# Graph attention on Trainium2: the softmax weights also in a PSUM bank of their own

## What is computed

```python
h = jnp.einsum('nf,fhd->nhd', x, W)            # 8 heads of 32
a_src = jnp.sum(h * att_src, axis=-1)
a_dst = jnp.sum(h * att_dst, axis=-1)
e = jax.nn.leaky_relu(a_src[src] + a_dst[dst], 0.2)
e_max = jax.ops.segment_max(e, dst, num_segments=N)
e_exp = jnp.exp(e - e_max[dst])
denom = jax.ops.segment_sum(e_exp, dst, num_segments=N)
msg = h[src] * (e_exp / (denom[dst] + 1e-16))[:, :, None]
out = jax.ops.segment_sum(msg, dst, num_segments=N)
```

## Time and profile before

| what | us |
|---|---|
| median of 3 runs | 3578.84 |
| the profiled execution's own time | 3577.81 |
| its span, first to last instruction | 3576.0 |
| PE busy (70%) | 2496.1 |
| POOL busy (56%) | 1996.6 |
| DVE busy (44%) | 1589.6 |
| ACT busy (37%) | 1310.4 |
| attention: first gather starts | 116.2 |
| attention: last gather starts | 1197.0 |

### The profile page before, as it was taken

The page is one execution under the profiler, slowest core; times in us unless marked ns, Lnnn a source line. Parts: engine busy times, 40 slices in busy tenths (PEclk is TensorE's granted clock), DMA queues, the critical chain, the costliest instruction groups (busy, mean ns, idle before and its releaser), DMA issues. The chain is left out here.

```text
span 3576.0 us, 51073 instructions
## 1 busy us (share of the span) xinstructions
PE 2496.1 (70%) x12468; PEld 1994.8 (56%) x12469; DVE 1589.6 (44%) x3485; ACT 1310.4 (37%) x2826; POOL 1996.6 (56%) x2005
## 2 busy tenths in 40 slices
PE   5466556666665552999924888878888878639993
PEld 4244444444444351888824676767777754427772
DVE  5455555555555582111156444444444454621114
ACT  5443333333333231544443333333222324624441
POOL 0577777777777356222204777777777730463331
PEclk9687888888887755999967999999999989769996
DMA  5444444444444235222255555555555520242226
GB/s 158 124 132 129 129 129 129 129 129 129 127 128 128 67 107 211 75 83 83 78 188 158 158 157 157 157 158 158 156 155 155 156 57 2 95 163 84 87 89 245
DMA packets 319924, 459.47 MB, mean 128 GB/s; under 512 B 56729, under 2 KB 213962, under 8 KB 319498
## 3 DMA queue, kind: packets, MB, share of 16 engines
q0 software_dynamic: 94560, 261.75, 24.6%
q1 hardware_dynamic: 212888, 180.18, 16.9%
q10 hardware_dynamic: 12276, 15.62, 1.3%
HBM read 376.96 MB, written 80.39 MB: 128 GB/s over the span
## 5 line engine op out<-in xcount | busy, mean ns | idle before, releaser
L604 POOL DMA_INDIRECT room<-h_table,src_idx x784 | 843.2, 1075 | 351.5 <-issue 238.2
L2170 POOL DMA_INDIRECT em_msg<-xn_table,src_idx x784 | 746.7, 952 | 337.2 <-issue 238.5
L1100 PE MATMUL at_ps<-room,at_member 128*128 128x264 f32 x1584 | 497.1, 468 | 74.1 <-DVE room L958 65.3
L2246 PE MATMUL em_pse<-em_We,em_attr_t 128*128 128x256 f32 x1552 | 398.4, 415 | 157.5 <-DVE em_msg L2194 157.5
L2194 DVE TENSOR_TENSOR em_msg<-em_pse,em_msg 128x1024 f32<-128x1024 f32 x196 | 230.9, 1220 | 548.1 <-DMA em_msg<-xn_table,src_idx 548.1
L2299 ACT ACTIVATE em_msg<-em_msg 128x1024 f32<-128x1024 f32 x196 | 207.2, 1057 | 681.5 <-DVE em_msg L2194 674.3
L2246 PEld LDWEIGHTS em_pse<-em_We,em_attr_t 128*128 128x128 f32 x1552 | 313.8, 207 | 226.3 <-DVE em_msg L2194 168.3
L1100 PEld LDWEIGHTS at_ps<-room,at_member 128*128 128x128 f32 x1584 | 342.9, 228 | 156.1 <-DVE room L958 82.4
L2253 PE MATMUL em_psa<-em_msg,em_member 128*128 128x256 f32 x1584 | 359.8, 381 | 3.2 <-DVE acc L2204 3.2
L2253 PEld LDWEIGHTS em_psa<-em_msg,em_member 128*128 128x128 f32 x1584 | 302.6, 191 | 44.4 <-DVE acc L2204 3.6
L1070 PE MATMUL at_pst<-ident,at_score 128*128 128x128 f32 x49 | 23.1, 472 | 349.3 <-DVE at_score L888 349.3
(11 more groups left out here) (397 smaller groups left out, 4048.1 us busy)
## 6 DMA issues: line engine op xcount, KB each, us to landing
em_attr<-in_edge_attr_dram SPq DMA_DIRECT2D x97, 512.0 KB, 4.2
room<-x_sorted SPq DMA_DIRECT2D x105, 258.0 KB, 2.7
at_dst_row<-dst_flat SPq DMA_DIRECT2D x98, 256.0 KB, 3.7
room<-h_table,src_idx POOLq DMA_INDIRECT x784
at_resets<-reset_flat SPq DMA_DIRECT2D x784, 8.0 KB
em_msg<-xn_table,src_idx POOLq DMA_INDIRECT x784, 2.8
room<-in_x_dram SPq DMA_DIRECT2D x12, 896.0 KB, 10.2
cn_rows<-y_table SPq DMA_DIRECT2D x5, 1792.0 KB, 10.2
```

What stands on the lines that cost most here:

```text
L604: pool.indirect_dma_start(msg[:, s, j, :], None, mem.h_table[:, :], bass.IndirectOffsetOnAxis(ap=mem.src_idx[:, c:c + 1].bitcast(u32), axi ...
L1100: ins = nc.tensor.matmul(ps_a[:, which, 0:MSG], member[which][:, j, :], msg[:, s, c, :], start=(j == 0), stop=(j == CB - 1))
L2170: pool.indirect_dma_start(msg[:, s, j, :], None, mem.xn_table[:, :], bass.IndirectOffsetOnAxis(ap=mem.src_idx[:, c:c + 1].bitcast(u32), ax ...
L2246: ins = nc.tensor.matmul(ps_e[h][:, j, :], attr_t[:, s % 2, c * P:(c + 1) * P], We[:, :], start=True, stop=True)
```

## The change

`ps_a` gives up its third bank, and `ps_w` takes it. ACT writes the weights twice: first into `ps_w` (its first 128 columns, chunk by chunk with the heads inside, semaphore `weight_out`), then into `msg` as before. `weigh` waits for the first copy, and takes its second operand from `ps_w` instead of from `msg`. The further windows' sums go to columns 8 to 271 of `ps_r`. New waits keep the order: `shift_scores` waits for the last weights in `msg`, PE's first product of a step does so too, and in the last step `spread_scale` waits for the first `weigh`.

```diff
-        ps_a = ctx.enter_context(nc.psum_tensor("at_ps", [P, 3, 512], fp32))
+        ps_a = ctx.enter_context(nc.psum_tensor("at_ps", [P, 2, 512], fp32))
+        ps_w = ctx.enter_context(nc.psum_tensor("at_psw", [P, 512], fp32))
...
+        sums = [ps_a[:, 0, 0:MSG], ps_a[:, 1, 0:MSG], ps_r[:, HEADS:HEADS + MSG]]
+        weight_row = ps_w[:, 0:P]
...
             def shift_scores(k, s, i):
                 dve.wait_ge(turned_back, k + 1)
+                if not isinstance(k, int) or k > 0:
+                    dve.wait_ge(weighted, k)
...
             def weigh(k, s, quarter):
-                dve.wait_ge(weighted, k + 1)
+                dve.wait_ge(weight_out, k + 1)
                 part = msg[:, s, quarter * HC:(quarter + 1) * HC, :].rearrange("p c (h w) -> p (c h) w", w=HW)
+                of_part = weight_row[:, quarter * HC * HEADS:(quarter + 1) * HC * HEADS]
                 nc.vector.tensor_tensor(part[:, :, 0:HD], part[:, :, 0:HD],
-                                        part[:, :, HD:HW].to_broadcast([P, HC * HEADS, HD]), ALU.mult).then_inc(msg_done, 1)
+                                        of_part.unsqueeze(2).to_broadcast([P, HC * HEADS, HD]), ALU.mult).then_inc(msg_done, 1)
...
             def spread_scale(k):
                 pe.wait_ge(scale_ready, k + 1)
                 pe.wait_ge(first_ready, 2 * k + 1)
+                if not has(1, k):
+                    pe.wait_ge(msg_done, 4 * k + 1)
...
             def first_half(k, s, p, half):
                 if half == 0:
                     pe.wait_ge(first_ready, 2 * k + p + 1)
                     pe.wait_ge(first_out, 2 * k + p + 1)
+                    if p == 0:
+                        pe.wait_ge(weighted, k + 1)
...
             def weights(k, s):
                 act.wait_ge(shifted, 2 * k + 2)
+                nc.scalar.activation(weight_row.rearrange("p (c h) -> p h c", h=HEADS), shift[:, :, :], ACT.Exp).then_inc(weight_out, 1)
                 nc.scalar.activation(weight_col(s), shift[:, :, :], ACT.Exp).then_inc(weighted, 1)
```

## The result

The changed kernel takes 3488.52 us (median of 4 runs, 3486.38 to 3492.24) against 3580.1 us for the kernel before (with one run more than above: 4 runs, 3577.42 to 3581.54): a ratio of 0.9746, 95% interval 0.9729 to 0.9763, and 91.6 us between the medians. Its profiled execution has a span of 3490.5 us.

What follows compares the result with a forecast made beforehand. POOL's row of attention gathers bounds the stage; 101.5 us of holds less 1.6, 7.2 and 0.6 gives 92 us off, a median of 3486.8 us, range 3479 to 3508, forecast chance 0.85.

Steps and rivals of the forecast that it cites:

- 101.5 us of holds: Attention's gathers: time the long ones carry beyond 784 x 0.946 us before the change, 99.9 of it to gain.
- the working: Attention's remaining holds: 1.6 us stay in the set-up, and 7.2 us fall anew under other SBUF-only DVE instructions.
- term for holds that fall anew: Attention steps: freed gather starts fall at random under marks, scans and shifts, 0.146 us a step, 7 us; bounds 0 to 68.
- the rule of the earlier trace: Gathers starting 0.04 us into an SBUF-only DVE instruction to 0.13 before its end lose what is left less 0.13.
- rival in which marks catch a gather in every step: Attention steps: holds change hands, both marks give 30 us back, 3510 us; over 20 us changing hands had chance 0.08.
- the sum's 92 us: Whole kernel: 101.5 us of holds less 1.6 set-up, 7.2 new holds and 0.6 at the end.
- second exponential: ACT in each attention step: 0 to 0.9 us, nearest 438 ns, hidden; without cover 21 us.
- gaining up to 70: Each weigh on DVE: 0 to 0.07 us longer, covered except the last two steps, 0.6 us at most.
- The last step's wait: Attention's last step: spread_scale waits for the first weigh while DVE has the second to run; nothing late, 0 us.
- DVE's cover: Attention steps: of DVE's 6.3 us waiting, over 4 are left after POOL gains 2, covering a longer weigh.
- the rival on the slower side: Weighs reading PSUM grow until DVE bounds the step, overtaking at 1.2 us more each; 3745 us at triple length; chance 0.03.

Runs made afterwards that it cites:

- the twins of one more instruction: Changed kernel plus one useless 128x1024 DVE product a step behind the last weigh: both operands in SBUF 3516.73 us (0.9803), second operand in PSUM 3492.52 us (0.9749).
- written but not read: Changed kernel with ACT's PSUM copy and the other new waits kept, but each weigh waiting for and reading msg again: 3583.88 us, ratio 0.9997.
- quarters 0 and 3 from SBUF: Changed kernel with weighs of quarters 1 and 2 reading PSUM, quarters 0 and 3 reading msg, all waiting for the copy into msg: 3540.19 us, ratio 0.9877.
- the runs with three and six more: Changed kernel plus three or six useless 1.2 us DVE products a step, all reading PSUM: 3542.97 us (0.9900) and 3731.87 us (1.0422).
- the added read of this case: Kernel with six more DVE instructions a step, plus one more block-word read a step, which left no instruction in the program: 3732.58 us, ratio 1.0423.

## Why the prediction came out

**The bound.** POOL's row of gathers was the stage. First to last start fell by 94.1 us and the median by 91.6; nothing else in the profile has a difference of that size.

**The mechanism.** Two operands in SBUF hold a gather that starts under them, one in PSUM doesn't: shown by undoing the read (0.9997), by moving the copy to SBUF (1.0001), and by the twins of one more instruction (47 gathers of 47 held against none).

The Trainium skill has this rule (SBUF — State Buffer, "Who interferes with whom": a DVE instruction with two SBUF inputs gets in the way of a GpSimd instruction that reads SBUF). The runs agree: the gather, which reads its index column from SBUF, takes 843.5 us in all with the weigh's operand in SBUF and 749.1 with it in PSUM.

**The size.** Of 101.5 us of holds 749.1 - 784 x 0.946 = 7.4 us are left, where the working had 7.2 + 1.6 = 8.8. The term for holds that fall anew was right in kind and near in size, though starts are not as random as it takes them to be (quarter 3 above). The marks are the largest part of what is left: 22 gathers end 0.82 us behind a mark and lose 3.2 us in all, by the rule of the earlier trace rows. Eleven end 0.75 us behind the scan with both operands in SBUF and lose 1.5 us. Eight gathers, into which a mark starts 0.36 to 0.45 us after their own start, take 0.02 to 0.10 us longer; that is not in the rule, and why is open. A gather behind a mark in the kernel after:

```profile
197.44 0.48 DVE L866 TENSOR_SCALAR at_first_t<-at_dst_row,node_of 128x1024 bf16<-128x1024 int16 x1
197.55 1.20 POOL L604 DMA_INDIRECT room<-h_table,src_idx  x1 [0.30 <-issue]
```

The rival in which marks catch a gather in every step, 3510 us with both marks, didn't come: 22 of 98 marks did. That was luck in the starts: 51 gathers start under a mark, but 22 of them within its first 0.07 us, where the marks held none, and 7 within its last 0.13.

The Trainium skill's rule for `tensor_scalar` in its two-port mode (same page and section) agrees with the 22 that were held; that the mark runs in this mode no row shows.

That the sum's 92 us meet the measured 91.6 so closely is luck too, since the runs of one kernel scatter by 6 us. Two errors cancel in it: the row of gathers gave 94.1 us where the sum had 92.7, and behind the last gather 3.0 us were lost where it had 0.6.

**ACT and the weigh.** The second exponential, bounded by 0 to 0.9 us, takes less than its twin. The kernel after, groups by line:

```profile
L1211 ACT ACTIVATE room<-at_shift 128x128 f32<-128x128 f32 x49 | 20.7, 422 | 0.0
L1210 ACT ACTIVATE at_psw<-at_shift 128x128 f32<-128x128 f32 x49 | 13.8, 281 | 139.3 <-DVE at_shift L940 126.0 <-DVE at_above L937 13.3
```

281 ns into PSUM, 422 into `msg`. It is the place and not the step of the output: with the first copy in SBUF, written with the same step as into PSUM, the exponential takes 437 ns:

```profile
L1211 ACT ACTIVATE at_weight_sb<-at_shift 128x128 f32<-128x128 f32 x49 | 21.4, 437 | 142.5 <-DVE at_shift L941 142.5
```

The weigh lost 6 ns instead of gaining up to 70. Both terms were hidden, and the run that writes without reading shows that together they cost nothing.

**Two terms that were wrong, of little weight.** *The last step's wait was put at 0.* DVE's `rescale` was hidden as said, but PE's products queue behind the scale's matmul: the first of them starts 1129.11 - 1127.25 = 1.86 us behind the first weigh's start, 1.38 before (1217.23 to 1218.61), 0.5 us that nothing covers behind the last gather. Another 2.4 us of the 3.0 there are the last 48 products, in 10.09 and 5.23 us against 9.04 and 3.83; the granted clock over those stretches was 0.73 and 0.72 against 0.81 and 1.00 (means between the two levels of 1.2 and 2.4 GHz). Stretches of PE, first the kernel before, then after (length, busy, count, granted clock):

```profile
1218.60:1227.70 9.10, 9.04 (x32) 0.81 0.01 2
1230.40:1234.30 3.90, 3.83 (x16) 1.00 0.00 0
```

```profile
1129.10:1139.20 10.10, 10.09 (x33) 0.73 0.01 2
1141.90:1147.20 5.30, 5.23 (x16) 0.72 0.00 0
```

What lowered it was not tried. Two runs with the same new wait, written but not read and the copy in SBUF, take 45.7 us from the last gather's start to the next stage at a granted clock of 0.80, where the kernel before takes 45.0 at 0.80, the kernel after 48.0 at 0.75, and quarters 0 and 3 from SBUF 43.5 at 0.85. So 0.5 to 0.7 us are the change's, and the rest comes together with a lower clock.

*DVE's cover was put at "over 4 us" a step.* All of its wait for the landing was counted as spare; the runs with three and six more show 2.3 to 2.6, and some 2.5 us a step of the wait are the sequencer's branches, word loads and jumps. (The cover is a little more than what is left, since DVE's wait for PE gives way too.) The forecast didn't hang on it, since the weigh didn't get longer, but the rival on the slower side did: its point of overtaking, 1.2 us more a weigh, would have been some 0.6. Six more instructions a step, 7.2 us, already make the kernel 4% slower than before.

## What to carry to other kernels

Where an engine's row of DMA issues is the bound, look at the spread of one issue, not at its mean: if a few take twice the middle one, and each ends a fixed time behind the same instruction of another engine, the price of that instruction is paid there and not on its own engine. Moving one operand of a DVE instruction to PSUM can then be worth more than making the instruction shorter. And an engine's wait for a landing is no measure of its spare time until the engine has been loaded: part of the wait can be time that its sequencer needs for branches, loads and the loop's jump. And a run that adds work must be looked up in its trace first: the added read of this case was never there.

## What was not expected of the hardware

An exponential of 128x128 numbers with a stepped output takes ACT 281 ns into PSUM, and 437 ns into SBUF with the same step. A DVE product with both operands in SBUF holds an indirect gather that starts from 0.03 us after its start (the earliest of the 47) to some 0.13 us before its end; a mark or a scan held none that started in its first 0.07 us. A DVE step in a loop of four, with DVE the bound, stands 1.75 to 1.85 us between its last and its first instruction, for its branches and the load of its block words (0.53 us), and 5.7 to 6.2 us where the loop jumps back; a branch that is not taken adds 0.2 us of it.
